# Projecting f in four column tiles, with one copy per unit for the energies' rows

## The reference, cut to what matters

```python
xf = x.reshape(B, C, N)                                  # B 4, C 256, N 4096
f = jnp.einsum('kc,bcn->bkn', w1, xf) + b1[None, :, None]   # 16 rows
energy = jnp.einsum('bkn,bkm->bnm', f, f)                # 4096 x 4096 per image
attention = jax.nn.softmax(energy, axis=-1)
out = jnp.einsum('bcm,bnm->bcn', xf, attention)
x = x + out.reshape(B, C, H, W) * 0.1
```

## Time and profile before

| | |
|---|---|
| median of three runs | 1972.63 us |
| the profiled execution's own time | 1972.71 us |
| its span | 1970.9 us |
| granted TensorE clock, mean | 0.98 |
| busy: PE, DVE, ACT, POOL | 97%, 79%, 72%, 62% |
| projections (line 390) | 4 at the head, 12 after it |
| DMA, mean rate | 68 GB/s |

### The profile page before, as it was taken

One profiled execution on the slowest core, in us unless ns is written; L12 is line 12 of the kernel. 1 busy time (PEld: TensorE's weight loads), 2 busy tenths in 40 slices (PEclk: granted clock), 3 DMA queues, 4 the chain that ended last, 5 costly groups with the idle time before them and its releaser, 6 DMA issues. The chain is left out here.

```text
span 1970.9 us, 40002 instructions
## 1 busy us (share of the span) xinstructions
PE 1904.9 (97%) x15232; PEld 1632.5 (83%) x15232; DVE 1565.6 (79%) x2149; ACT 1420.3 (72%) x2793; POOL 1215.7 (62%) x850
## 2 busy tenths in 40 slices
PE   6999999999999999999999999999999999999992
PEld 2799999998998899998999999988999999874440
DVE  5777777788877778778877777788888878858788
ACT  5777777777777777778777777777777777653335
POOL 4556555667855555567755656678655555649941
PEclk7899999999999999999999999999999999999996
DMA  6111111111211111013111110122011101236009
GB/s 215 41 51 60 54 40 35 32 64 57 71 51 59 62 41 32 30 59 107 54 62 58 34 30 30 32 85 64 31 31 32 32 32 73 86 120 239 1 39 388
DMA packets 58287, 133.67 MB, mean 68 GB/s; under 512 B 9328, under 2 KB 9328, under 8 KB 57584
## 3 DMA queue, kind: packets, MB, share of 16 engines
q1 hardware_dynamic: 58096, 131.10, 19.4%
HBM read 84.48 MB, written 33.62 MB: 60 GB/s over the span
## 5 line engine op out<-in xcount | busy, mean ns | idle before, releaser
L760 POOL CAST Ph<-P 128x1024 fp32r<-128x1024 f32 x496 | 725.2, 1462 | 625.4 <-ACT P L518 625.4
L610 DVE TENSOR_REDUCE nb<-scw 128x1 f32<-128x512 f32 (+1 forms) x988 | 680.6, 690 | 287.7 <-PE scw L408 283.2
L529 ACT ACTIVATE scw<-scw,nb 128x512 f32<-128x512 f32 (+1 forms) x988 | 655.7, 664 | 315.8 <-DVE nb L610 315.6
L426 PE MATMUL accb<-Ph,xh 64*128 64x512 f32 x2048 | 807.2, 394 | 1.4 <-ACT tb L539 1.3
L426 PE MATMUL acct<-Ph,xh 64*128 64x512 f32 x2048 | 804.7, 393 | 0.0
L426 PE MATMUL accb<-Ph,xl 64*128 64x512 f32 x2048 | 800.5, 391 | 0.0
L426 PE MATMUL acct<-Ph,xl 64*128 64x512 f32 x2048 | 796.3, 389 | 0.0
L620 DVE TENSOR_TENSOR Pl<-P,Ph 128x1024 fp32r<-128x1024 f32 x512 | 664.5, 1298 | 27.3 <-ACT Ph L523 15.9
L426 PE MATMUL acct<-Pl,xh 64*128 64x512 f32 x2048 | 635.7, 390 | 0.0
L426 PE MATMUL accb<-Pl,xh 64*128 64x512 f32 x2048 | 632.2, 388 | 0.0
L518 ACT ACTIVATE P<-ee 128x1024 f32<-128x1024 f32 x512 | 526.1, 1028 | 82.5 <-PE ee L399 67.0
(11 more groups left out here) (172 smaller groups left out, 1389.9 us busy)
## 6 DMA issues: line engine op xcount, KB each, us to landing
wk<-xt SPq DMA_DIRECT2D x32, 512.0 KB, 3.7
xres<-x SPq DMA_DIRECT2D x32, 512.0 KB, 3.8
x<-xres SPq DMA_DIRECT2D x32, 512.0 KB, 2.8
xr<-x SPq DMA_DIRECT2D x24, 512.0 KB, 8.7
out<-xr SPq DMA_DIRECT2D x24, 512.0 KB, 4.6
R<-rd SPq DMA_DIRECT2D x32, 256.0 KB, 3.1
xn<-x SPq DMA_DIRECT2D x16, 512.0 KB, 12.4
T<-xn SPq DMA_DIRECT2D x64, 100.0 KB
```

Of the source, the lines that this page charges most:

```text
L426: return pe.matmul(to[:, :], w[rows, g * GM + k, c * 128:(c + 1) * 128], p[rows, s, k * QC:(k + 1) * QC], start=g == 0 and i == 0, stop=g ...
L529: nc.scalar.activation(to, to, ACT.Exp, bias=nb[:, t % 2, w:w + 1], accum_out=bsum[:, t % 2, w:w + 1]).then_inc(bsum_done, 1)
L610: nc.vector.tensor_reduce(nb[:, t % 2, w:w + 1], of, AX.X, ALU.max, negate=True).then_inc(nmax_done, 1)
L760: nc.gpsimd.tensor_copy(Ph[:, e % RP, :], P[:, e % 2, :]).then_inc(ph_done, 1)
```

## The change

Pieces per unit: four instead of two, each with 32 output rows (w1 twice, for the high and the low part) on its own 32 columns of PE, so an image has two units, and after the head they run at step 5 of q = 2 and q = 4. At the head a unit is projected in two halves of two pieces. f_rows writes the scan's rows alone, per piece one DMA of 32 rows (high, low) and one of 16 (high again). e_rows, at step 13 after the head, then copies a unit's 48 rows from the scan's place to the energies' in one DMA. The ones are set once by DVE. At the head ACT issues the scan rows of tile 0, the last two pieces of x are loaded behind the first half unit's rows, and the three first blocks of transposed x go out right after the rows of the second half unit. In the last tile of an image POOL's joins and additions move from steps 4, 5, 11, 12 to 3, 6, 9, 12.

```diff
+FQ = 2 * KF
+FJ = 128 // FQ
+FU = N // (FJ * FW)
...
-            if t >= 0 and b < NB - 1 and 1 <= q <= FU and g == 5:
-                return (b + 1) * FU + q - 1
+            if t >= 0 and b < NB - 1 and q in (2, 4) and g == 5:
+                return (b + 1) * FU + q // 2 - 1
...
             if t % CH == CH - 1:
-                return (1, 2, 4, 5, 11, 12)
+                return (1, 2, 3, 6, 9, 12)
...
-            def f_rows(s):
+            def f_rows(s, h):
                 b, k = divmod(s, FU)
-                if b >= 2:
-                    sp.wait_ge(e_done, (b - 1) * CH * G)
-                sp.wait_ge(hl_done, s + 1)
-                for base, landed_in in ((S0, ts_in), (0, te_in)):
-                    for j in range(2):
-                        at = (2 * k + j) * 512
-                        sp.dma_start(T[b % 2][base:base + KS, at:at + 512].bitcast(F32),
-                                     hl[s % 2][j * S0:j * S0 + KS, :]).then_inc(landed_in[s % 2], 16)
+                sp.wait_ge(ones_done, 2)
+                sp.wait_ge(hl_done, 2 * s + h + 1 if s < FU else parts(s))
+                for j in (2 * h, 2 * h + 1):
+                    at = (FJ * k + j) * 512
+                    for row, rows in ((0, FQ), (FQ, KF)):
+                        sp.dma_start(T[b % 2][S0 + row:S0 + row + rows, at:at + 512].bitcast(F32),
+                                     hl[s % 2][j * FQ:j * FQ + rows, :]).then_inc(ts_in[s % 2][h], 16)
+
+            def e_rows(s):
+                b, k = divmod(s, FU)
+                if b >= 2:
+                    sp.wait_ge(e_done, (b - 1) * CH * G)
+                for h in range(2):
+                    sp.wait_ge(ts_in[s % 2][h], 64 * (s // 2 + 1))
+                at = slice(FJ * k * 512, FJ * (k + 1) * 512)
+                sp.dma_start(T[b % 2][0:KE, at].bitcast(F32), T[b % 2][S0:S0 + KE, at].bitcast(F32)
+                             ).then_inc(te_in[s % 2], 16)
...
+            f_rows(0, 0)
             for s in range(XP, SL):
                 load_piece(s)
-            scan_rows(0)
-            f_rows(0)
+            f_rows(0, 1)
+            for m in range(XB):
+                load_xt(m)
+            for h in range(2):
+                f_rows(1, h)
             scan_rows(1)
-            for s in range(1, FU):
-                f_rows(s)
-                load_xt(s - 1)
+            for s in range(FU):
+                e_rows(s)
             load_res(0)
...
                     if g == 8 and t >= 0 and projected(t, 5) is not None:
-                        f_rows(projected(t, 5))
+                        for h in range(2):
+                            f_rows(projected(t, 5), h)
+                    if g == 13 and t >= 0 and projected(t, 5) is not None:
+                        e_rows(projected(t, 5))
...
-            def project(s, bank):
-                for k in range(2 * s, 2 * s + 2):
+            def project(s, js, bank):
+                for j in js:
+                    k = FJ * s + j
                     pe.wait_ge(xp_in[k % XP], 16 * (k // XP + 1))
                 for c in range(CT):
-                    for j in range(2):
-                        mm = pe.matmul(bank[j * S0:(j + 1) * S0, 0:512], w1s[:, c, :], xp[(2 * s + j) % XP][:, c, :],
+                    for j in js:
+                        mm = pe.matmul(bank[j * FQ:(j + 1) * FQ, 0:512], w1s[:, c, :], xp[(FJ * s + j) % XP][:, c, :],
...
+            def first_rows():
+                act.wait_ge(hl_done, 1)
+                for to, at in ((0, 0), (1, 0), (2, 1)):
+                    act.dma_start(U[0][S0 + to * KF:S0 + (to + 1) * KF, :].bitcast(F32),
+                                  hl[0][at * KF:(at + 1) * KF, :]).then_inc(us_in[0], 16)
...
-                for s in HEAD_F.get(u, ()):
-                    copy_f(s, acc_t[s % 2])
+                for h in HEAD_F.get(u, ()):
+                    copy_f(h // 2, h % 2, acc_t[h % 2])
+                    if h == 1:
+                        first_rows()
...
+            for k in range(2):
+                nc.vector.memset(T[k][FQ:KS, :].bitcast(F32), 1.0).then_inc(ones_done, 1)
             dve.wait_ge(col_in, 16)
```

More of the change, by code:

```diff
@@ L155, in attention @@
         hl_done = sem("hl_done")
-        ts_in = [sem(f"ts_in{k}") for k in range(2)]
+        ts_in = [[sem(f"ts_in{k}_{h}") for h in range(2)] for k in range(2)]
         te_in = [sem(f"te_in{k}") for k in range(2)]
@@ L283, in scan_rows @@
                 if t < 2:
-                    src, row, s = hl[0], t * S0, slice(0, QC)
+                    src, row, s = hl[0], t * FQ, slice(0, QC)
                 else:
                     src, row, s = T[b % 2].bitcast(F32), S0, slice(q * QC, (q + 1) * QC)
-                for to, at in ((0, 0), (1, 2), (2, 1)):
+                for to, at in ((0, 0), (1, 0), (2, 1)):
                     sp.dma_start(U[t % 2][S0 + to * KF:S0 + (to + 1) * KF, :].bitcast(F32),
@@ L455, in _ @@
                     if u < G and u % 4 == 0:
-                        pe.wait_ge(ts_in[u // 4 % 2], 32 * (u // 8 + 1))
+                        pe.wait_ge(ts_in[u // 8][u // 4 % 2], 64)
                     elif u % (G * CH) == 0:
                         for k in range(2):
-                            pe.wait_ge(ts_in[k], 32 * (u // (G * CH) + 1) * FU // 2)
+                            for h in range(2):
+                                pe.wait_ge(ts_in[k][h], 64 * (u // (G * CH) + 1))
                 if 0 <= e < NG:
@@ L496, in _ @@
                         pe.wait_ge(p_done, e + 1)
-                        project(projected(t, g), ee)
-                        held[0] = (fp_done, projected(t, g) + 1)
+                        project(projected(t, g), range(FJ), ee)
+                        held[0] = (fp_done, parts(projected(t, g)))
             pe.wait_ge(p_done, NG)
@@ L539, in copy_bottom, with copy_f @@
                 nc.scalar.copy(tb[:, c, :], acc_b[c][:]).then_inc(bot_done, 1)
-            def copy_f(s, bank):
-                act.wait_ge(f_filled, 2 * (s + 1))
+            def copy_f(s, h, bank):
+                act.wait_ge(f_filled, FJ * s + (FJ if h is None else 2 * h + 2))
                 if s >= 2:
-                    act.wait_ge(hl_done, s - 1)
-                nc.scalar.activation(Fp[s % 2][0:S0 + KS, :], bank[0:S0 + KS, 0:512], ACT.Identity,
-                                     bias=col[0:S0 + KS, 0:1]).then_inc(fp_done, 1)
+                    act.wait_ge(hl_done, parts(s - 2))
+                rows = slice(0, 128) if h is None else slice(h * 64, (h + 1) * 64)
+                nc.scalar.activation(Fp[s % 2][rows, :], bank[rows, 0:512], ACT.Identity, bias=col[rows, 0:1]
+                                     ).then_inc(fp_done, 1)
+            def first_rows():
+                act.wait_ge(hl_done, 1)
+                for to, at in ((0, 0), (1, 0), (2, 1)):
+                    act.dma_start(U[0][S0 + to * KF:S0 + (to + 1) * KF, :].bitcast(F32),
+                                  hl[0][at * KF:(at + 1) * KF, :]).then_inc(us_in[0], 16)
             act.wait_ge(fill_done, 1)
@@ L571, in _ @@
                 if projected(t, g) is not None:
-                    copy_f(projected(t, g), ee)
+                    copy_f(projected(t, g), None, ee)
                 h = split_at(t, g)
@@ L705, in _ @@
                 e, u = n + 2, n + LAG
-                for s in HEAD_HL.get(u, ()):
-                    split_f(s)
+                for h in HEAD_HL.get(u, ()):
+                    split_f(h // 2, h % 2)
                 if g == 0 and t >= 1:
@@ L728, in _ @@
                 if projected(t, g) is not None:
-                    split_f(projected(t, g))
+                    split_f(projected(t, g), None)
                 if t == NT - 2 and 9 <= g < 9 + 3 * CT:
@@ L1098 @@
     w1, b1, w = (np.asarray(a) for a in (L0_conv_w1, L0_conv_b1, L1_conv_weights))
-    w1r = np.zeros((C, 64), f32)
+    w1r = np.zeros((C, FQ), f32)
     cols = np.zeros((128, 2), f32)
-    for r, low in enumerate((0, 1, 0)):
-        w1r[:, r * KF:(r + 1) * KF] = w1.T
-        for base in (0, S0):
-            rows = slice(base + r * KF, base + (r + 1) * KF)
+    for low in range(2):
+        w1r[:, low * KF:(low + 1) * KF] = w1.T
+        for j in range(FJ):
+            rows = slice(j * FQ + low * KF, j * FQ + (low + 1) * KF)
             cols[rows, 0] = b1
-            cols[rows, 1] = -1.0 if low else 0.0
-            cols[base + KE:base + KS, 0] = 1.0
+            cols[rows, 1] = -1.0 * low
     gb = np.concatenate([np.asarray(a).reshape(CT, 128).T for a in (L1_conv_gamma, L1_conv_beta)], axis=1)
```

38 lines of the change are left out of this document (20 added, 18 removed).

## The result

The changed kernel takes 1961.62 us (median of 5 runs, 1960.16 to 1962.48) against 1973.58 us before (1971.92 to 1973.88), a ratio of 0.994 [0.9927, 0.9953]: 12 us faster, 8.4 us short of the forecast of 1953.2. The profiled execution took 1960.16 us, its span 1958.2.

A forecast was written before the change was run, and what follows sets the result against it. TensorE, busy 97% of the span, was taken as the bound. 1972.7 - 12.0 (projection) - 6.5 (POOL's order) - 1.0 (head) = 1953.2 us; own range 1948 to 1958 (chance 0.55), wide range 1946 to 1963.

The forecast's parts named there:

- wide range: Whole kernel: 1946 to 1963 us, meant to leave out no more than 2 in 10, reaching to rivals on both sides.
- two rivals at 1959.7 and 1963.5: Image ends bound by ACT, so POOL's order gains nothing (chance 0.18); only two column tiles run at once (0.10).
- two-at-a-time rival: Projection: four column tiles share what two have, eight slots a unit, 1.7 of 12.0 us left: 1963.5 us, chance 0.10.
- Projection: Steady state: six projections of four column tiles in four slots replace twelve, 12.8 us instead of 24.8: -12.0 us.
- Rows of T in the steady state: SP's queue: 2 to 3 us of additional DMA issue per unit end inside the row shifts' wait for DVE: 0.
- POOL's order: Image's last tile: moving joins and adds off crowded steps wins two thirds of 9.7 us: -6.5, bounds -9.7 and +3.
- The sign named for it: Image's end: DVE's Pl subtraction at 1.2 to 1.6 us, not 2.3, in the last tile; pairs of tiles near 105 us.
- ACT's double step: Image's edge: accumulator copy and x copy in one ACT step, TensorE waiting 0.44 us at 493.05; forecast to stay.
- Head: Kernel's start: scan 0 to 1 us earlier, POOL some 5 us earlier but little seen: -1.0, between -2.5 and +2.
- memsets: Head: DVE's two memsets of 4096 columns take 6.9 us, ending before its first work at 11.11: 0.
- The step ahead of it: Head: transposed x's fourth load must wait for POOL behind the copies of T, giving back 2 us or more.
- Phase: Tiles of equal work: a phase between engines may tip in half of some twenty, 5.5 us either way; left at 0.

The follow-up runs named there:

- serial_pairs: Changed kernel with middle projections' column tiles issued in pairs, TensorE waiting for tiles 0 and 1 to finish before 2 and 3: 1974.15 us, ratio 0.9997.
- old_pool_order: Changed kernel with only POOL's order in an image's last tile set back to groups 1, 2, 4, 5, 11, 12: 1967.27 us, ratio 0.9964.
- head_and_ends: head_order plus POOL's joins and additions moved again in an image's last and first tiles: 1954.38 us, ratio 0.9896.
- early_xt: Changed kernel with the head's fourth block of transposed x loaded ahead of unit 1's rows of T, the fifth behind them: 1956.07 us, ratio 0.9908.
- head_order: Changed kernel with SyncE's head order changed: fourth to sixth blocks of transposed x earlier, residual and long copies last: 1956.83 us, ratio 0.9913.
- after_again: The changed kernel once more, unaltered, giving its second trace: 1962.28 us, ratio 0.9942 to the kernel before.
- pairs: Changed kernel with middle projections' column tiles issued two by two, without an added wait: 1962.84 us, ratio 0.9938.

## Why the prediction was right or wrong

*The total.* 1961.6 us lies in the wide range (1946 to 1963) but outside the forecast's own (1948 to 1958), between two rivals at 1959.7 and 1963.5 whose conditions do not hold: POOL's order did pay, and four column tiles did run at once. In the profiled execution the forecast is missed by 7.0 us, and the head alone misses by that. The upper end of the wide range was the two-at-a-time rival's and not worked out for the head, so that the total still fell inside it is luck.

*Projection, forecast -12.0, measured -12.3: right, and for its reason.* Four column tiles take the four slots of two. serial_pairs shows that it is this and not the number of stops. The attend follows 1.86 us after a unit's first matmul, as it did with two tiles (1.87). By the Trainium skill, "TensorE: Matmul & The Clock Gate", Part 3 (packing small matmuls), whose table gives 2.38 for three column tiles, the prediction estimated 2.17 us of slots for a unit in place of 1.72; the trace does not agree with that.

*Rows of T in the steady state, forecast 0: agrees.* From line 686 to line 686 the new copies, issued at steps 8 and 13, fall in the stretch behind a projection. Three of these six stretches, which had no projection before either, are as long as before to 0.01 us; the other three lost 1.96 to 2.09 us, as those without copies did (2.04 to 2.14).

*POOL's order, forecast -6.5, measured -5.1: the mechanism right, a fifth less than forecast.* old_pool_order gives it back alone. Two thirds of the excess were forecast; 1.7 of 3.1 us a pair went, a little over half. The sign named for it is there in part: in the first pair no subtraction of Pl (line 655) takes 2.30 us any more, where two did, but one takes 2.06 and four 1.75 or 1.76, above the 1.6 forecast; old_pool_order has two of 2.30 again. Of what stayed, head_and_ends got about 0.5 us more by POOL's order. ACT's double step stays, as forecast: TensorE waits 0.43 us for ACT's tb at 493.22, as it did 0.44 at 493.05, and the step around that wait takes 4.45 us as before (4.46), where plain ones take 3.24. Whether it goes when ACT's copies move was not tried.

*Head, forecast -1.0 with bounds of -2.5 and +2, measured +6.0 (+4.6 in the second trace): the step that failed.* Its first half holds: scan at 16.56, first block at 23.01, the memsets of 3.47 us hidden. The failed sentence is "The first attend hangs on step 0's energies, which wait for ACT's P until 59.25, and not on POOL, so little of that is seen". It misreads a row. These stand in the timeline of the kernel before:

```profile
53.91 0.76 PE L399 MATMUL ee<-U,T 50*128 50x512 f32 x1 [1.93 <-DMA U<-rows_t]
...
59.03 2.03 POOL L760 CAST Ph<-P 128x1024 fp32r<-128x1024 f32 x2
...
60.51 0.62 PE L426 MATMUL accb<-Ph,xh 64*128 64x512 f32 x1
```

Step 0's energies start at 53.91, when the row shift's DMA has landed; those at 59.25 are step 2's, two steps ahead of the attends. And POOL rounded the first P right behind its last split, from 59.03 to 60.07, 0.4 us before the first attend. So the first attend hung on two chains: through the first energies on the row shift, and, with 0.4 us to spare, on POOL. The change delayed both. Of the 4.6 us by which the first attend is late, 3.1 are the first energies' (56.97 instead of 53.91) and 1.5 are POOL's (the attend stands 8.1 us behind them instead of 6.6).

The step ahead of it, "I give 2 us of it back or more", set no upper end: the fourth block was not priced through SyncE's queue, where unit 1's rows (the second half from 28.25 on), the scan rows, the long copies, the residual and the energies' rows of U now stood ahead of it, until 38.57. The gap was 10.00 us, more than the 5.6 us by which POOL began earlier. The same lateness reached the row shift, as the eighth block, which waits for POOL, stands ahead of it in the queue: DVE's rows were there at 49.3, and the shift was issued at 53.06. early_xt shortens the gap to 3.51 us and has the shift issued at 49.59, as soon as DVE's rows are there, by moving two loads.

From the first attend to the tile's end another 1.4 us are lost (4.6 become 6.0). The granted clock fits that, though no run takes it alone: TensorE, idle for part of the wait, is at 0.50, its lower level of 1.2 GHz, over 57 to 65 us, at 0.53 over 65 to 72, and at 1.00 from 72 on; before it was 0.64 over 60 to 66 and 1.00 from 66 on. Over the twelve traces the two go together. At one end stands head_order: first attend at 63.96, clock 0.50 over 60 to 66 us and 1.00 from 67 on, and the tile ends 26.7 us after that attend. At the other stands serial_pairs: first attend at 65.83, clock 0.50 over 60 to 74 and 1.00 from 75 on, and the tile ends 30.0 us after it.

*Phase, forecast 0.* Such tips are there, with the same program: the tile from 729.3 to 781.0 us takes 51.72 in the changed kernel's trace, and the same tile 52.29 in after_again's. The runs of after_again spread from 1958.32 to 1966.08, so differences of less than 2 us between medians are not read here.

## What to carry to other kernels

A transfer moved in a queue has to be priced by the time at which its consumer runs dry, not by when it starts: list what stands ahead of each load, when its buffer comes free and when the data is wanted, to the last load. An engine that ends 0.4 us ahead of the path has 0.4 us to lose, so write the slack into the forecast before calling the engine off the path, and check of which step a row is. Transfers that two queues issue at about the same time can change places from one execution to the next. Matmuls with 32 output rows went four abreast here at the price of two; other shapes and types were not tried.

## What the runs showed of the hardware

Matmuls for other column tiles start ahead of matmuls that stand before them in the program: in pairs the third tile began 0.03 us behind the first two, whose next ones came 0.43 us after that. An order of matmuls alone does not keep column tiles apart; a wait does.

Behind two copies of 48 rows of 8 KB within one core's SBUF, SyncE's next two issues were held for 2.36 and 2.24 us; behind eight copies of rows of 2 KB with the same bytes they took 0.59 and 0.51.
